# The third routing group of a graph-attention and mixture-of-experts kernel: four tiles in one group instead of two groups of two

## What is computed

```python
# layer 1, on xn = layernorm(x)
h = xn @ W.T + b_W
e = (h @ a1)[:, None] + (h @ a2)[None, :] + b_a[0]
e = where(e > 0, e, 0.2 * e)
attention = softmax(where(adj > 0, e, -9e15), axis=1)
x = x + attention @ h
# layer 2, on xf = layernorm(x)
logits = xf @ Wr + br                      # 2048 x 64
topk_logits, topk_idx = top_k(logits, 2)
gates = softmax(topk_logits, axis=1)
for e in range(64):
    y = relu(xf @ W1[e] + b1[e]) @ W2[e] + b2[e]
    out = out + combine[:, e:e+1] * y      # combine: gates at topk_idx, else 0
x = x + out
```

## Time and profile before

| | |
|---|---|
| median of three runs | 266.3 us |
| the profiled execution's own time | 266.82 us |
| its span | 265.1 us |
| busy: TensorE, VectorE, ScalarE, GpSimd | 222.3, 210.0, 182.7, 155.5 us |
| chain that ended last: TensorE, VectorE, DMA, issue, GpSimd | 61%, 21%, 7%, 4%, 3% |
| of it L432, the scatters to the table | 2% |

### The profile page before, as it was taken

The page is one execution under the profiler, slowest core; times in us unless marked ns, Lnnn a source line. Parts: engine busy times, 40 slices in busy tenths (PEclk is TensorE's granted clock), DMA queues, the critical chain, the costliest instruction groups (busy, mean ns, idle before and its releaser), DMA issues.

```text
span 265.1 us, 6251 instructions
## 1 busy us (share of the span) xinstructions
PE 222.3 (84%) x1863; PEld 212.4 (80%) x1863; DVE 210.0 (79%) x596; ACT 182.7 (69%) x434; POOL 155.5 (59%) x195
## 2 busy tenths in 40 slices
PE   1493999999996999889946469999999999999840
PEld 1353999999996999789925369999999999999730
DVE  6899999999999989999586117888886666676365
ACT  2758979999876889695635238778767777777400
POOL 5780000533578838688787563446888888865600
PEclk9999599999998999999995559999999999999995
DMA  5989764497757861139811132222369410100067
GB/s 150 225 153 172 139 116 82 129 260 200 206 145 133 282 219 80 43 113 422 357 44 53 35 102 62 63 67 66 83 231 305 154 42 31 40 27 30 24 209 276
DMA packets 11120, 36.89 MB, mean 139 GB/s; under 512 B 2256, under 2 KB 2832, under 8 KB 10320
## 3 DMA queue, kind: packets, MB, share of 16 engines
q0 software_dynamic: 5232, 14.98, 24.7%
q1 hardware_dynamic: 5424, 21.11, 23.1%
q10 hardware_dynamic: 432, 0.40, 0.5%
HBM read 39.36 MB, written 5.51 MB: 169 GB/s over the span
## 4 chain that ended last, share of the span: by engine, by line
PE 61%; DVE 21%; DMA 7%; issue 4%; POOL 3%; SPq 1%; ACT 1%; POOLq 0%; DVEq 0%
PE bank L1157 17%; PE bank L1169 16%; PE bank L1050 13%; PE bank L1026 9%; DVE arena L760 5%; DVE arena L754 4%; DMA xs<-in_x 2%; DMA arena<-result 2%; POOL table L432 2%; PE bank L1146 2%; DVE arena L745 1%; PE bank L1069 1%; DVE idx L784 1%; DVE hot L790 1%; DMA rows_in<-table,arena 1%
## 5 line engine op out<-in xcount | busy, mean ns | idle before, releaser
L1050 PE MATMUL bank<-arena 128*128 128x130 f32 x512 | 62.2, 278 | 0.0
L1157 PE MATMUL bank<-arena 128*128 x384 | 60.5, 282 | 0.1
L1050 PEld LDWEIGHTS bank<-arena 128*128 128x128 f32 x512 | 60.3, 194 | 0.2 <-DVE xs L768 0.2
L1169 PE MATMUL bank<-w2s,arena 128*128 x384 | 58.8, 276 | 0.2 <-issue 0.2
L1157 PEld LDWEIGHTS bank<-arena 128*128 128x128 f32 x384 | 51.6, 196 | 0.6 <-issue 0.3
L1169 PEld LDWEIGHTS bank<-w2s,arena 128*128 128x128 f32 x384 | 50.6, 192 | 0.6 <-issue 0.6
L918 DVE SCALAR_TENSOR_TENSOR arena<-bank,arena 128x128 f32 x96 | 33.6, 350 | 21.5 <-PE bank L1169 20.2
L661 ACT ACTIVATE arena<-bank,arena 128x128 f32<-128x128 f32 x96 | 35.2, 367 | 18.3 <-PE bank L1157 16.9
L432 POOL DMA_INDIRECT table<-rows_in,pos x32 | 40.1, 1254 | 10.0 <-issue 8.0
L1026 PE MATMUL bank<-ident,arena 128*128 128x128 f32 x256 | 34.2, 291 | 9.5 <-DVE arena L760 9.5
L911 DVE TENSOR_SCALAR arena<-bank,arena 128x128 f32<-128x128 f32 x96 | 33.3, 346 | 10.1 <-PE bank L1157 9.9
(11 more groups left out here) (196 smaller groups left out, 278.2 us busy)
## 6 DMA issues: line engine op xcount, KB each, us to landing
arena<-in_adj POOLq DMA_DIRECT2D x16, 512.0 KB, 6.6
w2s<-in_w SPq DMA_DIRECT2D x8, 768.0 KB, 4.5
arena<-in_w SPq DMA_DIRECT2D x6, 1024.0 KB
arena<-in_w SPq DMA_DIRECT2D x4, 512.0 KB, 5.3
w2s<-in_w SPq DMA_DIRECT2D x4, 512.0 KB, 3.9
xs<-in_x SPq DMA_DIRECT2D x4, 256.0 KB, 6.3
arena<-result SPq DMA_DIRECT2D x2, 512.0 KB, 4.3
arena<-result SPq DMA_DIRECT2D x4, 256.0 KB, 5.9
```

The lines of the kernel that those rows point to most:

```text
L1050: ins = pe.matmul(OB[t % 2][:, 0:D + 2], pt_r[:, t % 2, j, :], h[:, j, :], start=(j == 0), stop=(j == T - 1))
L1157: ins = pe.matmul(hp(p, b), w1u[:, p % UW, P * b:P * b + P], xT_all[:, bass.ds(column, P)], start=True, stop=True)
L1169: ins = pe.matmul(yp(p), hT[:, p % UH, b, :], w2s[:, bass.ds(u, 1), b, :].rearrange("p e d -> p (e d)"), start=(b == 0), stop=(b == HB - 1))
```

## The change

The groups become tiles 0 to 3, 4 to 7, 8 to 11, 12 and 13, 14, 15: the old groups 2 (tiles 8, 9) and 3 (tiles 10, 11) are one. `EARLY` falls to 2, so the new group 2 is routed at the written-out places that the old group 3 had; the groups behind it are numbered one lower and keep their places on TensorE. On VectorE each `top2` and `place` behind the loop is put one `residual` later or earlier as shown. On GpSimd tile 3 is sent one step earlier, tile 4 in step 13, tile 5 in step 14, and tiles 9 to 11 in another order against `rstd_of`.

```diff
--- before.py
+++ after.py
@@ -17,14 +17,14 @@
     HB = HID // P
     TOPK = 2
     GRP = 4
-    START = [0, 4, 8, 10, 12, 14, 15, T]
+    START = [0, 4, 8, 12, 14, 15, T]
     NG = len(START) - 1
     SIZE = [START[q + 1] - START[q] for q in range(NG)]
-    SLOT = [0, GRP, 0, 2, GRP, GRP + 2, GRP + 3]
+    SLOT = [0, GRP, 0, GRP, GRP + 2, GRP + 3]
     COUNTED = 2
     LAST = [START[q + 1] - 1 for q in range(NG)]
-    PLACED = [(0, 0, 10), (0, 1, 11), (0, 2, 12), (0, 3, 13), (1, 4, 14), (1, 5, 15), (1, 6, 15), (1, 7, 15)]
-    EARLY = 3
+    PLACED = [(0, 0, 10), (0, 1, 11), (0, 2, 12), (0, 3, 12), (1, 4, 13), (1, 5, 14), (1, 6, 15), (1, 7, 15)]
+    EARLY = 2
     NORMED = [(5 + 2 * i, 2 * i) for i in range(5)]
     LNS = [(t, t + 2) for t in range(0, T - 2, 2)] + [(T - 2, T - 1), (T - 1, T)]
     CB = 4
@@ -459,12 +459,12 @@
                         counts(q)
             rstd_of(6)
             place(2, 8)
+            place(2, 9)
             rstd_of(7)
-            place(2, 9)
-            place(3, 10)
+            place(2, 10)
+            place(2, 11)
             rstd_of(8)
-            place(3, 11)
-            for q in range(4, NG):
+            for q in range(3, NG):
                 for t in range(START[q], START[q + 1]):
                     place(q, t)
             pool.wait_ge(s_rows, 1)
@@ -620,7 +620,7 @@
                         norm(t)
                         norm(t + 1)
                 if s == T - 1:
-                    route_a(3)
+                    route_a(2)
                 if s >= 1:
                     evac(s - 1)
                 for q in range(EARLY):
@@ -630,19 +630,19 @@
                     norm(T - 6)
                     norm(T - 5)
             deviation(T - 3)
-            route_b(3)
+            route_b(2)
             norm(T - 4)
             norm(T - 3)
             evac(T - 1)
+            route_a(3)
+            norm(T - 2)
             route_a(4)
-            norm(T - 2)
+            route_b(3)
+            deviation(T - 1)
+            route_b(4)
+            norm(T - 1)
             route_a(5)
-            route_b(4)
-            deviation(T - 1)
             route_b(5)
-            norm(T - 1)
-            route_a(6)
-            route_b(6)
 
             for b0, b1_ in ((0, 16), (16, NB)):
                 act.activation(y_all[:, b0:b1_, :],
@@ -786,7 +786,7 @@
                 dve.wait_ge(s_lg, q + 1)
                 link(dve.tensor_copy(idxf[:, rows, :], idx8[:, 0:n, 0:TOPK]))
                 if q >= COUNTED:
-                    dve.wait_ge(s_cnt, min(q // 2, COUNTED))
+                    dve.wait_ge(s_cnt, min(q - 1, COUNTED))
                 link(dve.tensor_tensor(hot[:, :, kept(q), :],
                                        iota_e[:, :].rearrange("p (k g e) -> p k g e", k=1, g=1).to_broadcast([P, TOPK, n, E]),
                                        idxf[:, rows, :].rearrange("p g (k e) -> p k g e", e=1).to_broadcast([P, TOPK, n, E]), ALU.is_equal))
@@ -848,17 +848,16 @@
                         place(q)
             leaky(T - 1)
             residual(T - 3)
+            top2(2)
+            residual(T - 2)
             place(2)
             top2(3)
-            residual(T - 2)
+            residual(T - 1)
             place(3)
             top2(4)
-            residual(T - 1)
             place(4)
             top2(5)
             place(5)
-            top2(6)
-            place(6)
 
             c_e, side_e, w_e = (num[:, k:k + 1] for k in range(3))
             first_e, last_e, last_g = (mark[:, k:k + 1] for k in range(3))
@@ -1033,18 +1032,18 @@
                     if t == LAST[q] + 3:
                         route_a(q)
                 if t == T - 2:
-                    route_b(3)
+                    route_b(2)
                 if t == T - 1:
-                    route_a(4)
+                    route_a(3)
                 for j in range(T):
                     b = j // CB
                     for q in range(EARLY):
                         if j == T // 4 and t == LAST[q] + 3:
                             route_b(q)
                     if t == T - 1 and j == 8:
-                        route_b(4)
+                        route_b(3)
                     if t == T - 1 and j == 12:
-                        route_a(5)
+                        route_a(4)
                     if j % CB == 0:
                         pe.wait_ge(s_ea, 4 * t + b + 1)
                     ins = pe.matmul(OB[t % 2][:, 0:D + 2], pt_r[:, t % 2, j, :], h[:, j, :], start=(j == 0), stop=(j == T - 1))
@@ -1096,15 +1095,15 @@
                     if s == LAST[q] + 4:
                         route_c(q)
                 if s == T - 3:
-                    route_a(3)
+                    route_a(2)
                 if s == T - 2:
-                    route_c(3)
+                    route_c(2)
+            route_c(3)
+            route_b(4)
             route_c(4)
+            route_a(5)
             route_b(5)
             route_c(5)
-            route_a(6)
-            route_b(6)
-            route_c(6)
 
 
             pe.wait_ge(s_set, 1)
```

## The result

The changed kernel takes 272.4 us (median of four runs, 271.85 to 273.01) against 266.3 us; the ratio is 1.0218, 95% interval 1.0181 to 1.0256, so 4.8 to 6.8 us. The forecast was 271.2, its range 268.5 to 272.5. The profiled execution took 272.85 us, its span is 271.0.

What follows compares the result with a forecast made beforehand. GpSimd's full queue, sending 16 issues from tile 8 to the padding rows, was taken as the bound; late norms 2.4 plus late position step 2.5 gave 266.3 + 4.9 = 271.2 us, range 268.5 to 272.5.

Steps and rivals of the forecast that it cites:

- The queue is the bound: GpSimd's queue, tile 8's first issue to the padding rows: 16 issues and two statistics, 21.9 us, nothing saved by the change.
- The position step late: VectorE, four-tile position step behind tile 14's residual, with the same GpSimd queue behind it: 2.5 of the 4.9 us.
- The norms late: ScalarE, norms of tiles 10 and 11 wait for rstd_of(5), starting at 117.9 instead of 114.73: about 2.4 us.
- The attention product, 3.64: TensorE, attention product of tile 14 behind the logits of four tiles: 3.64 us, ending at 127.85 instead of 125.44.
- hidden behind ScalarE: TensorE's transposes of tiles 8 to 11 wait for the late norms, done about 121.5, claimed to cost nothing.
- one more pass: Rival: tile 4's second GpSimd issue falls inside a VectorE pass, rstd_of(5) at 118.5, +0.9 more, 272.1 us; chance 0.13.
- the pair tables: Rival: pair tables become last, moving over 2.66 us more than the gathers; +0.9, 272.1 us; chance 0.07.
- Tile 15's spread: Spread ready at about 140.6, its turn in GpSimd's queue at 141.7: covered by 1.1 us.
- The 2.66 of cover: ScalarE waited 2.66 us for the first gathered rows after its weight copies; forecast to cover 1.7, with 1.0 left.

## Why the prediction was right, and what it missed

- **The queue is the bound, and its 16 issues take 21.9 us**: right, 21.92. With rstd_of(7) first a gap of 3.44 on TensorE cost nothing.
- **The position step late, 2.5 of the 4.9**: right. With the norms on time and the clock up (VectorE waits for the statistic), what is left over the kernel before is 44.39 - 42.08 = 2.3; the move alone in the kernel before makes the stretch 2.2 longer.
- **The norms late, 2.4**: right in size, 117.02 - 105.36 = 11.7 behind the scores pass of tile 14 instead of 8.6. With the clock kept up the stretch is 46.72, another 2.3 above 44.39. But the reason given was half of it: the prediction counted the passes' move forward only as a gain that the other engines might not use, and put the lateness on the two issues ahead of the statistic. With tile 5 back at step 15 the closed-up passes alone made the norms late.
- **"The attention product, 3.64"** is the term that was mis-sized: it measured 5.45. I had found TensorE's waits ahead of it ("hidden behind ScalarE") and costed them at nothing, where they cost the clock. Keeping TensorE busy gives the term: 1.65. The sum 4.9 + 1.65 is 6.55; 6.3 was measured in the stretch, 6.1 in the medians.
- **The range**: that 272.4 lies inside, 0.1 below the upper end, is luck. The 272.5 was set by two late rivals, one more pass and the pair tables. Neither came; a loss that the prediction did not have filled their place.
- **One more pass**: did not come; tile 4's second issue started 0.01 behind the start of a pass and took 0.96. The mask compare does hold what starts inside it, but not an issue that the scores pass ahead of it has let go: tile 4's first issue ended at 108.54, 0.90 behind the scores pass and only 0.29 behind the mask compare (107.56 to 108.25), and tile 5's first ended 0.82 behind a leaky pass, which no compare follows.
- **The pair tables**: nearly. Tile 15 was normalised at 143.44 (143.2 forecast) but transposed only at 144.67, 8.05 later than before instead of 6.6: on TensorE the count of tile 14 stands ahead of it, at 144.25 behind a wait of 1.86, and the product of tile 15 and tile 14's logits before that ran at half clock (1.94 for the product's last quarter, 1.06 before). ScalarE's weight copies came at 159.72, 8.65 later, against 5.57 for the first gather. The 2.66 of cover are gone: the copy of the first gathered rows follows without a wait, at 160.66. The first expert product still is only 5.6 late.
- **Tile 15's spread**, forecast 1.1 ahead of its turn in the queue, came 0.65 ahead (141.91 against 142.56).

The three steps 2.3, 2.3 and 1.65 lie between four stretches, so that they add up to the 6.29 by themselves proves nothing. The check is another one: in the kernel before, the late position step alone costs 2.16 and the loop order alone, norms and clock together, 4.46. That is 6.6 of the stretch, against 6.29 for the whole change.

## What to carry to other kernels

Ask of each short instruction on a shared queue not only when it is ready but beside what it would then run: the small instructions between two long passes were the window in which it ran at its own price, and the change removed them. Work merged into larger groups waits for its last member, and on a queue without slack everything behind starts there. And a wait of TensorE that is off the path is not free where it makes the next product run at half clock.

## What the runs showed of the hardware

- A GpSimd product, addition, copy or indirect-DMA issue that starts inside a two-input VectorE pass of 128 x 2048 does not go on until the pass ends: a copy of 0.37 took 2.3 to 2.4, a product of 0.19 up to 2.2, an issue of 0.96 up to 3.2. In the twelve traces every product, addition and copy from 0.16 us in and every indirect issue from 0.12 in was held, the issues to 0.8 to 1.0 behind the end of the pass. An issue up to 0.08 in, or ahead of the pass, was not (0.96 to 1.05); at 0.09 both occur, 1.05 before (86.59) and 3.18 with tile 5 back at step 15 (86.19). Between two passes back to back a held issue gets through (1.90 in the rows above).
- A statistic is caught earlier. Started with the pass (tile 5 back at step 15, 110.61 against 110.58) it took 2.83; its own 0.58 to 0.72 reaches further into the pass, but what in it is held wasn't separated.
- A one-input bf16 pass of 128 x 2048 (the mask compare, 0.69) holds too: an addition of 0.30 that started 0.09 in took 0.76 to 0.77 in every trace, a copy of 0.37 that started 0.18 in took 0.76.
- A direct DMA issue of GpSimd (L379) is not held: started 0.38 into such a pass, at 29.94 before, it took 0.53.
- TensorE's granted clock fell to 0.50 behind two waits of 1.38 and 1.10 us with 2.4 us of work between them, and also behind 0.58 and 1.10 (tile 5 back at step 15). It stayed at 1.00 when nine useless products filled most of both waits.
